# A mixture of experts that gathers its rows by tile of slots instead of scattering them into slots

## The chip, the cores and the metric

One program on one core of a Trainium2 chip. The metric is the device time of one execution in microseconds (us). The engines are TensorE (PE, whose weight loads have a row of their own, PEld), VectorE (DVE), ScalarE (ACT), GpSimd (POOL) and SyncE (SP, which here only issues DMAs).

## What is computed

A decoder of twelve sublayers over 8 sequences of 256 tokens with 256 features (2048 tokens in all). The change concerns the third sublayer, a mixture of 8 experts of which each token uses two. Cut to what matters:

```
S, C, K, E = 2048, 640, 2, 8                 # tokens, slots of an expert, choices, experts
probs = softmax(xf @ Wg)                     # 2048 x 8
top_vals, top_idx = top_k(probs, K)
onehot = one_hot(top_idx.T.reshape(-1), E)   # first choices of all tokens, then second choices
loc = place of each (token, choice) in its expert: cumsum(onehot) - 1
keep = loc < C
gates = top_vals * keep;  gates /= max(gates.sum(-1), 1e-9)
buf[e, loc] = xf[token]                      # 8 experts x 640 slots x 256
hid = buf @ W_in;  a, g = split(hid);  hid = gelu(a) * g
out_e = hid @ W_out
y[token] = sum over its two choices of gates * out_e[e, loc]
```

The sublayer is followed by a residual sum and a normalisation of each token's row.

## The kernel before

The sublayers run one after another, each in a block of its own (`turn`); x stays in SBUF twice, `x_tok` (a token in each partition, 16 tiles of 128 tokens) and `x_feat` (transposed). Within a block every engine has its own program in a fixed order, and semaphores connect them. `then(...)` makes VectorE wait for the end of the instruction it wraps before the next.

`mixture_top2` has three stretches. (1) Routing: TensorE makes the logits, VectorE the softmax, the two best experts, one-hot rows `hot` and, by two products with `ones16` and `before16` and a scan, the place of each of the 4096 (token, choice) pairs in its expert; at the end `slot` (128 partitions x 2 choices x 16 tiles of tokens) holds 640 * expert + place, or a number out of bounds where the expert is full (L1688, which raises `slot_done`). (2) The rows travel. ScalarE has copied x into `sheets`, two copies with rows of 258 words: 256 of x, the gate, and the pair's number. GpSimd issues 32 indirect DMAs (L1506), one for each choice and tile of tokens, that scatter 128 rows each into `rows_in` in HBM; SyncE waits until all 32 have landed (L1465) and loads the slots, one expert of five tiles a DMA (L1473), three experts ahead, into `xt`. (3) Experts: the 40 tiles of 128 slots go in 16 parts (`PARTS`, 3 and 2 tiles of an expert in turn). `turn_row` transposes a tile (L1528), ScalarE stores it in `xT` (L1605); `hidden` multiplies by `w_in` (L381 is the line of the helper `mm`), ScalarE makes gelu (L1613), VectorE the product with the gate half (L1695); `outer` multiplies by `w_out`, VectorE scales by the row's gate (L1703) and raises `out_stored`, and GpSimd scatters the 128 rows to `rows_back`, a row for each (token, choice) pair (L1513). In a part TensorE does `hidden` of part q, `outer` of part q-1 and `turn_row` of part q+1, so that a tile is transposed about five tiles before its own `outer`. A ring of `RING` = 4 buffers `y` holds results until their scatter has landed. When all 40 have, SyncE reads `rows_back` by token, two rows each, and the residual follows.

`rows_in` has to hold something in slots that no pair takes: the first sublayer's SyncE program writes 40 tiles of `ident` and of `blank` (whose last word is a pair number out of bounds) into it (L916, L918), then zeros into `rows_back` (L921), then issues the loads of the masks (L1284). `rows_in` is filled again in the fourth sublayer for the second mixture (`mixture_top3`), which is not changed but for the count that it waits for.

An fp32 matmul of the program is two matmul instructions in the trace, with a weight load each; a transpose is one.

## Time and profile before

| | us |
|---|---|
| median of 3 runs | 2690.61 (2690.55 to 2693.39) |
| the profiled execution | 2685.21 |
| its span, from first to last instruction | 2683.4 |
| TensorE busy | 2294.8 (86%) |
| VectorE busy | 1425.6 (53%) |
| ScalarE busy | 1041.7 (39%) |
| GpSimd busy | 700.3 (26%) |
| mean granted TensorE clock | 0.921 |
| the mixture's block | 235.1 to 561.1 |

What lies around the span is 1.8 us. The span is a sequence of blocks, so a microsecond taken from the path within one block moves all that follows.
### The profile page before, as it was taken

To read this page: it belongs to the slowest core of one execution; us is meant where nothing else is said; L and a number is where in the kernel's file an instruction comes from. 1 tells how busy PE (TensorE), PEld (TensorE's weight loads), DVE (VectorE), ACT (ScalarE), POOL (GpSimd) and SP (SyncE) were. 2 spreads that over 40 slices of the span, in tenths; PEclk is the share of its full clock that TensorE was granted. 3 is DMA by queue.
4 is the path that set the end of the run, shared out by engine and by line. 5 is a ranking of instruction groups with operands and counts; after the bars stand their busy time and mean duration, and the time that the engine had idled before them with its cause. 6 is when DMAs were issued, how large, how long until landed. Compare 5 with 4: busy or idle time off the path is not lost. (4 is left out here: it accounts for less than half of the span.)

```text
span 2683.4 us, 38848 instructions
## 1 busy us (share of the span) xinstructions
PE 2294.8 (86%) x12968; PEld 1648.2 (61%) x12968; DVE 1425.6 (53%) x4229; ACT 1041.7 (39%) x2653; POOL 700.3 (26%) x670
## 2 busy tenths in 40 slices
PE   7994499888869829995699799698999898999898
PEld 5773377665547518883388566464566676466676
DVE  3565022266758764556133667454776443777454
ACT  3442111145526510045044266343666432666432
POOL 1013311110024342311644100563433101433111
PEclk9996799989969959997899899799999999999899
DMA  9123211184000010030254311400000000000000
GB/s 235 33 94 139 78 51 43 39 155 23 1 6 1 1 49 11 1 131 6 95 153 120 116 25 25 159 1 32 1 1 1 1 1 1 1 1 1 20 24 20
DMA packets 112242, 127.38 MB, mean 47 GB/s; under 512 B 46515, under 2 KB 100021, under 8 KB 110256
## 3 DMA queue, kind: packets, MB, share of 16 engines
q1 hardware_dynamic: 103312, 103.91, 14.5%
q0 software_dynamic: 8736, 20.99, 2.1%
q8 instruction: 109, 1.79, 0.3%
q14 instruction: 85, 0.70, 0.1%
HBM read 79.93 MB, written 47.90 MB: 48 GB/s over the span
## 5 line engine op out<-in xcount | busy, mean ns | idle before, releaser
L381 PE MATMUL bank<-weights,work 128*128 128x256 f32 (+5 forms) x1768 | 467.3, 399 | 52.0 <-POOL work L2489 35.0
L381 PE MATMUL bank<-work,weights 128*128 128x256 f32 (+3 forms) x1680 | 407.5, 403 | 20.0 <-DVE work L4710 12.6
L381 PEld LDWEIGHTS bank<-weights,work 128*128 128x128 f32 (+2 forms) x1768 | 315.8, 192 | 151.5 <-issue 66.3
L381 PEld LDWEIGHTS bank<-work,weights 128*128 128x128 f32 (+1 forms) x1680 | 299.5, 189 | 101.2 <-DVE work L4710 16.1
L765 POOL TENSOR_TENSOR work<-work,minus_half 128x2 f32<-128x2 f32 x96 | 69.7, 726 | 837.0 <-DVE work L758 837.0
L381 PE MATMUL bank<-weights,x_feat 128*128 128x512 f32 (+2 forms) x576 | 213.0, 503 | 16.0 <-ACT weights L4286 10.0
L790 ACT COPY x_feat<-bank 128x512 f32<-128x512 f32 x80 | 46.5, 584 | 324.1 <-PE bank L782 323.7
L381 PEld LDWEIGHTS bank<-weights,x_feat 128*128 128x128 f32 x576 | 106.8, 198 | 74.8 <-issue 50.4
L4310 ACT ACTIVATE work<-work 128x128 f32<-128x128 f32 (+1 forms) x256 | 137.0, 543 | 1.7 <-DVE work L4397 1.7
L381 PE MATMUL bank<-x_feat,weights 128*128 128x256 f32 (+3 forms) x400 | 117.5, 471 | 19.9 <-PEq L232 15.2
L1695 DVE TENSOR_TENSOR work<-bank,work 128x384 f32<-128x384 f32 (+1 forms) x64 | 31.4, 491 | 189.5 <-ACT work L1613 189.5
L381 PE MATMUL bank<-weights 128*128 128x256 f32 (+1 forms) x560 | 125.9, 380 | 1.5 <-DVE weights L4427 0.9
L381 PEld LDWEIGHTS bank<-weights 128*128 128x128 f32 x560 | 105.0, 192 | 16.7 <-ACT weights L4334 1.3
L381 PEld LDWEIGHTS bank<-x_feat,weights 128*128 128x128 f32 (+1 forms) x400 | 78.1, 213 | 48.1 <-issue 22.8
L381 PE MATMUL bank<-work 128*128 128x256 f32 (+3 forms) x326 | 73.3, 362 | 29.5 <-ACT work L2875 7.8
L782 PE MATMUL bank<-ident,x_tok 128*128 128x128 f32 x320 | 61.4, 327 | 38.1 <-DVE x_tok L773 36.1
L4720 DVE SCALAR_TENSOR_TENSOR work<-bank,weights,work 128x256 f32<-128x256 f32 x96 | 45.6, 482 | 85.1 <-ACT work L4658 84.0
L4122 POOL TENSOR_TENSOR work<-work,minus_half 128x8 f32<-128x8 f32 x32 | 52.4, 1636 | 145.2 <-DVE work L4441 145.2
L1513 POOL DMA_INDIRECT rows_back<-work x40 | 38.9, 971 | 195.2 <-DVE work L1703 191.5
L4658 ACT ACTIVATE work<-bank,weights 128x256 f32<-128x256 f32 x80 | 37.9, 474 | 126.5 <-PE bank L381 126.3
L4389 DVE CUSTOM_DVE_ANT_0 work<-bank,work 128x128 f32<-128x128 f32 (+1 forms) x256 | 75.9, 352 | 16.9 <-PE bank L4173 16.9
L1613 ACT ACTIVATE work<-bank 128x384 f32<-128x384 f32 (+1 forms) x64 | 28.0, 437 | 146.3 <-PE bank L381 146.3
(465 smaller groups left out, 4688.8 us busy)
## 6 DMA issues: line engine op xcount, KB each, us to landing
weights<-in_weights SPq DMA_DIRECT2D x1, 12296.0 KB
weights<-in_weights SPq DMA_DIRECT2D x1, 9360.0 KB
weights<-in_weights SPq DMA_DIRECT2D x1, 8488.0 KB
work<-rows_in SPq DMA_DIRECT2D x62, 129.0 KB
rows_in<-ident SPq DMA_DIRECT2D x2, 3968.0 KB, 43.7
weights<-rows_back SPq DMA_DIRECT2D x8, 768.0 KB, 5.1
work<-rows_in SPq DMA_DIRECT2D x8, 645.0 KB, 4.2
rows_in<-ident SPq DMA_DIRECT2D x2, 2560.0 KB, 34.4
```

The source lines that it names most:

```text
L381: ins = nc.tensor.matmul(out, lhsT, rhs, start=(i == 0), stop=(i == len(pairs) - 1))
L765: nc.gpsimd.tensor_tensor(t.rstd[:, n, :], t.rstd[:, n, :], K.minus_half[:, 0:2], ALU.pow).then_inc(K.S.rstd_done, 1)
L782: ins = nc.tensor.transpose(K.bank[bank][:, (2 * k + i) * P:(2 * k + i + 1) * P], K.x_tok[:, 2 * b + i, k * P:(k + 1) * P], K.ident[:])
L790: copy(K.x_feat[:, :, b * L:(b + 1) * L], K.bank[bank][:, :].rearrange("p (k t) -> p k t", k=KT)).then_inc(K.S.xT_stored, 1)
L1513: nc.gpsimd.indirect_dma_start(K.rows_back, bass.IndirectOffsetOnAxis(ap=to, axis=0), y[:, r, :], None, bounds_check=TOP * T - 1, oob_is_e ...
L1613: nc.scalar.activation(gelu[:, at % 2, 0:n], K.bank[2 * (at % 2)][:, 0:n], ACT.Gelu).then_inc(S.gelu_done, 1)
L1695: nc.vector.tensor_tensor(hT[:, q % 2, m, 0:n], K.bank[2 * (at % 2) + 1][:, 0:n], gelu[:, at % 2, 0:n], ALU.mult).then_inc(S.inner_stored, 1)
L4122: nc.gpsimd.tensor_tensor(rk, norm[:, 1, :], K.minus_half[:, 0:H], ALU.pow).then_inc(S.rk_done, 1)
L4310: ins = nc.scalar.activation(probs[:, u % 3, s, at:at + width], probs[:, u % 3, s, at:at + width], ACT.Exp, bias=bias[:, u % 2, i, s:s + 1 ...
L4389: ins = nc.vector.tensor_tensor_reduce(probs[:, u % 3, s, at:at + width], K.bank[SM[s]][:, at:at + width], seen[:, at:at + width], 1.0, -3 ...
L4658: nc.scalar.activation(gelu[:, n % 2, :], K.bank[n % RING][:, L:2 * L], ACT.Gelu, bias=W["b1"][:, layer, HT + f:HT + f + 1]).then_inc(S.ge ...
L4720: nc.vector.scalar_tensor_tensor(out=hid[rows, b % 2, f, :], in0=K.bank[n % RING][rows, 0:L], scalar=W["b1"][rows, layer, f:f + 1], in1=ge ...
```

## The change

Rows are no longer scattered into slots. At the start of the block SyncE writes x twice into `slots_in` in HBM, a row for each (token, choice) pair (2 DMAs of 2048 KB, semaphore `x_doubled`). VectorE goes on from `slot`: it splits the number into the tile of slots (0 to 39) and the place in the tile (0 to 127), and makes one-hot rows of both, `in_tile` (128 x 32 x 40) and `in_slot` (128 x 32 x 128), and `value`, which is `in_tile` times the pair's number plus one (`ids`) and times its gate (`share`). TensorE adds up 32 products of `in_slot` (as weights) and `value` (80 columns) in one bank: the result says for each place and tile which pair sits there and with what gate. Six small VectorE operations turn it into `weight`, `source` (row to read, 0 where the slot is empty) and `target` (row to write, out of bounds where empty), and raise `slot_done`. GpSimd then gathers: one indirect DMA for each tile of slots from `slots_in` into one of `AHEAD` = 8 buffers `xt`; eight at once, and from then on gather j+8 behind scatter j. SyncE loads no slots, ScalarE makes no copies of x, and the fill of `rows_in` in the first sublayer is gone. Semaphores that even blocks share are assigned anew. The gate comes from `weight`.

```
     def sync(sp):
         follow_weights(sp, K, 0)
-        fill = K.rows_in[0:40 * P, :].rearrange("(n p) c -> p n c", p=P)
-        for k in range(KT):
-            sp.dma_start(fill[:, :, k * P:(k + 1) * P], K.ident[:].unsqueeze(1).broadcast_to([P, 40, P])
-                         ).then_inc(K.rows_cleared, 16)
-        sp.dma_start(fill[:, :, D:D + 2], K.blank[:].unsqueeze(1).broadcast_to([P, 40, 2])
-                     ).then_inc(K.rows_cleared, 16)
         sp.wait_ge(S.zeros_done, 1)
         sp.dma_start(K.rows_back[0:2 * T, :].rearrange("(n p) d -> p n d", p=P),
                      zeros.unsqueeze(1).broadcast_to([P, 2 * TILES, D])).then_inc(K.back_cleared, 16)
...
-    place, none, share, slot = A(TOP, TILES), A(TOP, TILES), A(TOP, TILES), A(TOP, TILES, dt=U32)
+    place, none, share = A(TOP, TILES), A(TOP, TILES), A(TOP, TILES)
+    slot, low, ids = A(TOP, TILES, dt=I32), A(TOP, TILES), A(TOP, TILES)
+    columns, tiles_of, found = A(P), A(E * EACH), A(2, E * EACH)
+    source, target, weight = A(E * EACH, dt=U32), A(E * EACH, dt=U32), A(E * EACH)
     tail = tail_buffers2(A)
     at = A.at
-    sheets = A(TOP, TILES, ROW)
+    in_tile, in_slot, value = A(TOP * TILES, E * EACH), A(TOP * TILES, P), A(TOP * TILES, 2, E * EACH)
     A.at = at
-    xt, xT, hT = A(SETS, EACH, ROW), A(2, KT, WIDE), A(2, HT, WIDE)
...
+    doubled = K.slots_in[0:TOP * T, :].rearrange("(i p c) d -> c p i d", p=P, c=TOP)
         def _(sp):
+            for c in range(TOP):
+                sp.dma_start(doubled[c], K.x_tok[:]).then_inc(K.x_doubled, 16)
             follow_weights(sp, K, 2)
-            sp.wait_ge(K.scattered_top2, 16 * TOP * TILES)
-            sp.wait_ge(S.x_copied, TOP)
-            slots = K.rows_in[0:E * CAPACITY, :].rearrange("(e i p) c -> e p i c", e=E, p=P)
-            for e in range(E):
-                if e >= SETS:
-                    for r in range(RING):
-                        done = len(range(r, EACH * (e - SETS + 1), RING))
-                        sp.wait_ge(K.sent_top2[r], 16 * done)
-                sp.dma_start(xt[:, e % SETS, :, :], slots[e]).then_inc(slots_loaded[e % SETS], 16)
...
-                ins = nc.gpsimd.iota(sheets[:, c, :, D + 1:D + 2].rearrange("p i a -> p (i a)").bitcast(U32),
-                                     pattern=[[TOP * P, TILES]], base=c, channel_multiplier=TOP)
-            ins.then_inc(S.pool_step, 1)
+                nc.gpsimd.iota(ids[:, c, :], pattern=[[TOP * P, TILES]], base=c + 1, channel_multiplier=TOP,
+                               allow_small_or_imprecise_dtypes=True)
+            nc.gpsimd.iota(tiles_of, pattern=[[1, E * EACH]], base=0, channel_multiplier=0,
+                           allow_small_or_imprecise_dtypes=True)
+            nc.gpsimd.iota(columns, pattern=[[1, P]], base=0, channel_multiplier=0,
+                           allow_small_or_imprecise_dtypes=True).then_inc(S.pool_step, 1)
+            def gather(j):
+                if j >= AHEAD:
+                    p.wait_ge(S.row_turned, j - AHEAD + 1)
+                nc.gpsimd.indirect_dma_start(xt[:, j % AHEAD, :], None, K.slots_in,
+                                             bass.IndirectOffsetOnAxis(ap=source[:, j:j + 1], axis=0),
+                                             bounds_check=TOP * T - 1, oob_is_err=False).then_inc(K.gathered[j % AHEAD], 16)
+
+            def scatter(j):
+                p.wait_ge(S.out_stored, j + 1)
+                nc.gpsimd.indirect_dma_start(K.rows_back, bass.IndirectOffsetOnAxis(ap=target[:, j:j + 1], axis=0),
+                                             y[:, j % RING, :], None, bounds_check=TOP * T - 1, oob_is_err=False
+                                             ).then_inc(K.sent_top2[j % RING], 16)
+
+            p.wait_ge(S.pool_step, 4)
+            p.wait_ge(K.back_cleared, 16)
+            p.wait_ge(K.x_doubled, 16 * TOP)
             p.wait_ge(S.slot_done, 1)
-            p.wait_ge(S.x_copied, TOP)
-            p.wait_ge(S.pool_step, 4)
-            p.wait_ge(K.rows_cleared, 48)
-            p.wait_ge(K.back_cleared, 16)
-            for c in range(TOP):
-                for i in range(TILES):
-                    nc.gpsimd.indirect_dma_start(K.rows_in, bass.IndirectOffsetOnAxis(ap=slot[:, c, i:i + 1], axis=0),
-                                                 sheets[:, c, i, :], None, bounds_check=E * CAPACITY - 1,
-                                                 oob_is_err=False).then_inc(K.scattered_top2, 16)
-            for j, (q, i) in enumerate(tiles):
-                r = j % RING
-                p.wait_ge(S.out_stored, j + 1)
-                to = row_of(q, i)[:, D + 1:D + 2].bitcast(U32)
-                nc.gpsimd.indirect_dma_start(K.rows_back, bass.IndirectOffsetOnAxis(ap=to, axis=0), y[:, r, :], None,
-                                             bounds_check=TOP * T - 1, oob_is_err=False).then_inc(K.sent_top2[r], 16)
+            for j in range(AHEAD):
+                gather(j)
+            for j in range(len(tiles)):
+                scatter(j)
+                if j + AHEAD < len(tiles):
+                    gather(j + AHEAD)
...
+                pe.wait_ge(K.gathered[j % AHEAD], 16 * (j // AHEAD + 1))
                 if j >= 2:
                     pe.wait_ge(S.row_stored, j - 1)
                 for k in range(KT):
-                    ins = nc.tensor.transpose(K.bank[6 + j % 2][:, k * P:(k + 1) * P], row_of(q, i)[:, k * P:(k + 1) * P],
+                    ins = nc.tensor.transpose(K.bank[6 + j % 2][:, k * P:(k + 1) * P], xt[:, j % AHEAD, k * P:(k + 1) * P],
                                               K.ident[:])
...
+            for n in range(TOP * TILES):
+                if n % TILES == 0:
+                    pe.wait_ge(S.row_found, n // TILES + 1)
+                ins = nc.tensor.matmul(K.bank[5][:, 0:2 * E * EACH], in_slot[:, n, :],
+                                       value[:, n, :, :].rearrange("p a j -> p (a j)"), start=n == 0,
+                                       stop=n == TOP * TILES - 1)
+            ins.then_inc(S.aux_done, 1)
             pe.wait_ge(S.slot_done, 1)
...
-            nc.scalar.copy(sheets[:, 0, :, 0:D], K.x_tok[:]).then_inc(S.x_copied, 1)
             a.wait_ge(S.max_done, 1)
             nc.scalar.activation(prob, prob, ACT.Exp).then_inc(S.probs_done, 1)
-            nc.scalar.copy(sheets[:, 1, :, 0:D], K.x_tok[:]).then_inc(S.x_copied, 1)
             for j in range(PARTS[0][2]):
...
-            for c in range(TOP):
-                ins = nc.vector.tensor_tensor(sheets[:, c, :, D:D + 1], share[:, c, :].unsqueeze(2), total.unsqueeze(2),
-                                              ALU.mult)
-            then(ins)
+            then(nc.vector.tensor_tensor(share, share, total.unsqueeze(1).broadcast_to([P, TOP, TILES]), ALU.mult))
             far = float(2 * E * CAPACITY)
             then(nc.vector.tensor_scalar(none, none, -far, far, ALU.mult, ALU.add))
             then(nc.vector.tensor_tensor(place, place, none, ALU.add))
             then(nc.vector.scalar_tensor_tensor(out=place, in0=by_rank(wheref), scalar=float(CAPACITY), in1=place,
                                                 op0=ALU.mult, op1=ALU.add))
-            nc.vector.tensor_copy(slot, place).then_inc(S.slot_done, 1)
+            then(nc.vector.tensor_copy(slot, place))
+            then(nc.vector.tensor_scalar(slot, slot, P - 1, None, ALU.bitwise_and))
+            then(nc.vector.tensor_copy(low, slot))
+            then(nc.vector.tensor_tensor(place, place, low, ALU.subtract))
+            then(nc.vector.tensor_scalar(place, place, 1.0 / P, None, ALU.mult))
+            both, ranks = [P, TOP * TILES, E * EACH], "p c i -> p (c i)"
+            then(nc.vector.tensor_tensor(in_tile, tiles_of.unsqueeze(1).broadcast_to(both),
+                                         place.rearrange(ranks).unsqueeze(2).broadcast_to(both), ALU.is_equal))
+            for n, x in enumerate((ids, share)):
+                nc.vector.tensor_tensor(value[:, :, n, :], in_tile, x.rearrange(ranks).unsqueeze(2).broadcast_to(both),
+                                        ALU.mult)
+            for c in range(TOP):
+                nc.vector.tensor_tensor(in_slot[:, c * TILES:(c + 1) * TILES, :],
+                                        columns.unsqueeze(1).broadcast_to([P, TILES, P]),
+                                        low[:, c, :].unsqueeze(2).broadcast_to([P, TILES, P]), ALU.is_equal
+                                        ).then_inc(S.row_found, 1)
+            v.wait_ge(S.aux_done, 4)
+            inverse = K.bank[5][:, 0:2 * E * EACH].rearrange("p (a j) -> p a j", a=2)
+            nc.vector.tensor_copy(weight, inverse[:, 1, :])
+            then(nc.vector.tensor_scalar(found[:, 0, :], inverse[:, 0, :], -0.75, 0.25, ALU.add, ALU.max))
+            then(nc.vector.tensor_copy(source, found[:, 0, :]))
+            then(nc.vector.tensor_scalar(found[:, 1, :], inverse[:, 0, :], 0.5, float(4 * T), ALU.is_lt, ALU.mult))
+            then(nc.vector.tensor_tensor(found[:, 1, :], found[:, 1, :], found[:, 0, :], ALU.add))
+            nc.vector.tensor_copy(target, found[:, 1, :]).then_inc(S.slot_done, 1)
...
-                nc.vector.tensor_scalar(y[:, j % RING, :], K.bank[4 + j % 2][:, 0:D], row_of(q, i)[:, D:D + 1], None,
+                nc.vector.tensor_scalar(y[:, j % RING, :], K.bank[4 + j % 2][:, 0:D], weight[:, j:j + 1], None,
...
-        K.slots_in = nc.dram_tensor("slots_in", (6400, D), F32, kind="Internal").ap()
+        K.slots_in = nc.dram_tensor("slots_in", (2 * T, D), F32, kind="Internal").ap()
```

How the instructions stand. VectorE, where the routing ends and the experts begin, before:

```order
L1680 TENSOR_TENSOR work<-work 128x16 x2
L1684 TENSOR_SCALAR work<-work 128x32
L1685 TENSOR_TENSOR work<-work 128x32
L1686 SCALAR_TENSOR_TENSOR work<-work 128x32
L1688 CAST work<-work 128x32
L1695 TENSOR_TENSOR work<-bank1,work 128x384
```

VectorE, from the same place on, of the changed kernel (bank 5 is where the 32 products are added up):

```order
L1682 CAST work<-work 128x32
L1683 TENSOR_SCALAR work<-work 128x32
L1684 CAST work<-work 128x32
L1685 TENSOR_TENSOR work<-work 128x32
L1686 TENSOR_SCALAR work<-work 128x32
L1688 TENSOR_TENSOR work<-work 128x1280
L1691 TENSOR_TENSOR work<-work 128x32x40 x2
L1694 TENSOR_TENSOR work<-work 128x2048 x2
L1700 COPY work<-bank5 128x40
L1701 TENSOR_SCALAR work<-bank5 128x40
L1702 CAST work<-work 128x40
L1703 TENSOR_SCALAR work<-bank5 128x40
```

Behind these stand two more of 128x40 and then the first product of the experts: 15 instructions more between the CAST of `slot` and the experts than before.

TensorE at the same place, before:

```order
L1571 MATMUL bank1<-ident,work 128x128 x4
L381 MATMUL bank3<-work 128x256
L381 MATMUL bank2<-work 128x256
L1528 MATMUL bank6<-ident,work 128x128 x2
L1528 MATMUL bank7<-ident,work 128x128 x2
```

and of the changed kernel:

```order
L1563 MATMUL bank1<-ident,work 128x128 x4
L381 MATMUL bank3<-work 128x256
L381 MATMUL bank2<-work 128x256
L1573 MATMUL bank5<-work 128x80 x32
L1520 MATMUL bank6<-ident,work 128x128 x2
L1520 MATMUL bank7<-ident,work 128x128 x2
```

The 32 products stand in a row between the routing's last products and the first transposes; from there on the two orders are the same.

GpSimd's whole list of row transfers before:

```order
L1506 DMA rows_in<-work 7936x258 x32
L1513 DMA rows_back<-work 6144x256 x40
L765 TENSOR_TENSOR work<-work,minus_half 128x2 x8
```

and its beginning in the changed kernel:

```order
L1485 IOTA work 128x128
L1490 DMA work<-slots_in,work 128x256 x8
L1496 DMA rows_back<-work 6144x256
L1490 DMA work<-slots_in,work 128x256
L1496 DMA rows_back<-work 6144x256
```

Eight gathers in place of 32 scatters stand ahead of the experts, and 32 more alternate with the first 32 of the 40 scatters of results.

## Rows read from the trace of the kernel before

**Rows 1.** The page's part 1: busy us (share of the span) xinstructions

```profile
PE 2294.8 (86%) x12968; PEld 1648.2 (61%) x12968; DVE 1425.6 (53%) x4229; ACT 1041.7 (39%) x2653; POOL 700.3 (26%) x670
```

**Rows 2.** Windows: engines' busy us, granted clock, DMA share, GB/s, by stretch

```profile
core 0: us, PE busy (x) PEld busy (x) DVE busy (x) ACT busy (x) POOL busy (x), PEclk, DMA share, GB/s
...
253.50:296.60 43.10, 0.00 (x0) 0.00 (x0) 0.00 (x0) 0.00 (x0) 31.36 (x32) 0.50 0.27 97
296.60:303.20 6.60, 1.81 (x7) 1.04 (x7) 0.00 (x0) 1.19 (x4) 0.00 (x0) 0.50 0.86 267
303.20:530.40 227.20, 219.19 (x906) 165.37 (x906) 50.80 (x104) 41.21 (x102) 38.86 (x40) 0.99 0.10 34
```

**Rows 3.** Timeline from `slot` to the experts: start us, us, engine, line, operation

```profile
253.26 0.18 DVE L1688 CAST work<-work 128x32 uint32<-128x32 f32 x1
254.35 1.22 POOL L1506 DMA_INDIRECT rows_in<-work  x1 [17.78 <-DVE work L1688]
255.88 0.98 POOL L1506 DMA_INDIRECT rows_in<-work  x1 [0.30 <-issue]
...
294.20 0.97 POOL L1506 DMA_INDIRECT rows_in<-work  x1 [0.30 <-issue]
296.63 1.50 SPq L1473 DMA_DIRECT2D work<-rows_in  x3
...
300.89 1.81 PE L1528 MATMUL bank<-ident,work 128*128 128x128 f32 x6 [53.09 <-DMA work<-rows_in]
...
303.16 7.21 PE L381 MATMUL bank<-work,weights 128*128 128x384 f32 x16 [0.46 <-ACT work L1605]
```

**Rows 4.** VectorE by width: timeline; last row busy us, mean ns

```profile
249.03 0.42 DVE L1666 TENSOR_TENSOR work<-work 128x256 f32<-128x256 f32 x1
...
253.01 0.21 DVE L1686 SCALAR_TENSOR_TENSOR work<-work 128x32 f32<-128x32 f32 x1
...
308.35 0.56 DVE L1695 TENSOR_TENSOR work<-bank,work 128x384 f32<-128x384 f32 x1 [54.92 <-ACT work L1613]
...
L3698 DVE TENSOR_REDUCE work<-weights 128x512 f32<-128x4096 f32 x1 | 4.4, 4416 | 0.0
```

**Rows 5.** Timeline of short TensorE pairs, at the lower and the upper clock

```profile
229.02 1.06 PE L782 MATMUL bank<-ident,x_tok 128*128 128x128 f32 x4
...
198.59 1.05 PE L381 MATMUL bank<-work 128*128 128x120 f32 x8
...
543.52 0.60 PE L782 MATMUL bank<-ident,x_tok 128*128 128x128 f32 x4
```

**Rows 6.** Windows where the granted clock (behind POOL) changes

```profile
304.00:306.00 2.00, 2.00 (x5) 1.09 (x4) 0.00 (x0) 0.41 (x1) 0.00 (x0) 0.50 0.00 0
306.00:307.00 1.00, 1.00 (x4) 0.56 (x3) 0.00 (x0) 0.00 (x0) 0.00 (x0) 0.60 0.00 0
...
532.00:533.00 1.00, 0.00 (x0) 0.00 (x0) 0.00 (x0) 0.00 (x0) 0.00 (x0) 0.54 0.90 315
```

**Rows 7.** The line of the scatters of results (L1513)

```profile
L1513 POOL DMA_INDIRECT rows_back<-work x40: 971/971/973, 320.7 to 528.2; - x40
...
DMA to landing us min/median/max: 2.0/2.4/4.1
```

**Rows 8.** Timeline: first result scaled; transposes of tile 8

```profile
319.47 0.48 DVE L1703 TENSOR_SCALAR work<-bank,work 128x256 f32<-128x256 f32 x1 [0.89 <-PE bank L381]
...
337.96 0.38 PE L1528 MATMUL bank<-ident,work 128*128 128x128 f32 x2
```

**Rows 9.** The DMAs' issues: count, KB each, us to landing

```profile
rows_back<-work SPq DMA_DIRECT2D x1, 4096.0 KB, 25.7
...
x_saved<-x_tok SPq DMA_DIRECT2D x1, 2048.0 KB, 9.1
```

**Rows 10.** Waits in 0 to 120 us: us in total, times, longest

```profile
PEld bank L381 <- DMA weights<-in_weights: 12.2, 1, 12.2
...
POOL x_tok L941 <- DMA ctx_feat<-in_ctx_feat: 5.2, 1, 5.2
```

40 lines of the change are left out of this document (17 added, 23 removed).

## The prediction

> **What bounds the kernel now.** TensorE is busy for 86% of the span [rows 1], so first I looked for places where it is not. The table of windows over this block shows one: from 253.5 to 296.6 us no TensorE, VectorE or ScalarE instruction runs, only GpSimd with its 32 scatters, and in the next 6.6 us TensorE is busy for 1.8 [rows 2]. From 303.2 on the experts keep TensorE at 219 of 227 us. So within this block two things set the time: the experts' products, which the change leaves as they are, and the way from the finished slot numbers to the first product of an expert. The timeline lays that way out [rows 3]: `slot` is ready at 253.26 + 0.18 = 253.44; the first scatter starts 0.91 later, the second 1.53 after it, the rest 1.28 apart (38.32 us over 30); the last starts at 294.20; SyncE issues the load of the slots 2.43 later; transposes begin at 300.89 and the first expert's product at 303.16. That is 49.7 us from `slot`, all of it on the path, for TensorE's transposes wait for nothing else (53.1 us, the one wait on a DMA). The question is what the new way from 253.44 costs.
>
> **Step 1, VectorE makes one-hot rows.** The nearest rows for small operations are those of 32 columns: 0.18 us and 0.04 to the next, so 0.22 [rows 4]. Four of them: 0.9. The gate's two operations become one, worth under 0.1, left out. The wide ones go by their length: 256 columns take 0.42, 384 take 0.56, and the one long row, 4096 columns, 4.42 [rows 4]. Between them the slope is 1.04 to 1.09 ns for a column, with 0.15 us on top. One of 1280 columns is 1.5 us and there are three (`in_tile`, two `value`): 4.5; one half of `in_slot`, 2048 columns, is 2.3. TensorE may begin when the first half stands: 253.44 + 0.9 + 4.5 + 2.3 + 0.1 of gaps = 261.2. The second half ends at 263.5, under TensorE's first. Bounds: the long row is a reduction and not two operands that are spread out, but 4.42 / 4096 leaves little room below; above, I allow 2 us.
>
> **Step 2, TensorE adds up 32 products.** That is 64 weight loads of 128 columns and 64 matmuls of 80. No row has this shape. The nearest have 128 and 120 columns behind loads of 128: four take 0.60 us at the upper clock, eight take 1.05, so one more costs 0.11; four take 1.06 at the lower clock, so about 0.21 [rows 5]. With 128 columns loaded and 128 streamed in 0.107, load and stream run beside each other; with 80 streamed the load of 128 should set the pace, still 0.107. The clock: TensorE has then been idle for some 13 us and starts at the lower level. In the trace it began at 300.89 and was at 1.2 GHz until within 306 to 307 (mean 0.60 there) [rows 3, 6], 5.5 us. The same again gives 25 pairs at 0.21 (5.3 us), then 39 at 0.107 (4.2), and 0.2 until the last is out: 9.7, ending at 270.9. Ends: 7 us if the 80 streamed columns set the pace (0.067, by the 0.107 for 128), 13.7 + 0.2 if the clock stays low.
>
> **Step 3, six small VectorE operations** of 40 columns, in a chain: 6 x 0.22 = 1.3, so `slot_done` at 272.2.
>
> **Step 4, the gathers.** The trace has no gather; the nearest row is the scatter of as many rows. From VectorE's end to the first indirect DMA 0.91 us, to the third another 1.53 + 1.28 [rows 3]: it starts at 275.9. A scatter lands 2.0 to 4.1 us after its issue, 2.4 in the median [rows 7]: 278.3. Then two transposes, a copy by ScalarE and the product; before, three tiles took 303.16 - 300.89 = 2.3 for that, and now two of them are done while the third travels. I take 1.2 (between 0.8 and 2.3). First product at 279.5 instead of 303.2.
>
> **The gain is 23.7 us.** What else moves:
> - The two copies of x to HBM. They are issued at the block's start, 235.1. Copies of 2048 KB have landed after 9.1 us, one of 4096 KB after 25.7 [rows 9]; 235.1 + 18.2 = 253 or 235.1 + 25.7 = 261 stands against a need at 272.2. Cost nothing; covered by the routing and steps 1 to 3, with 11 us to spare, and from then on one for one. Behind them on SyncE's queue stands the load of the fourth sublayer's weights, needed at 561.
> - ScalarE's two copies of x (3.6 us each) lay beside the routing: nothing. Three more iotas on GpSimd lie there too.
> - The fill of `rows_in` in the first sublayer, 5 MB, goes. Nothing there waits for a DMA after 12.2 us but GpSimd's first bias addition, 5.2 us, for an input that was issued ahead of the fill [rows 10]; TensorE and VectorE wait for no transfer. It gains nothing, and zeros and masks land earlier than they are needed.
> - In the experts GpSimd issues 72 indirect DMAs instead of 40. Results are scaled from 319.47 on [rows 8], one in 5.3 us on average (to 527.0, 39 steps), and two issues take 2 x 1.28 = 2.6. A gather stands behind the scatter of eight tiles earlier: that of tile 8 may be issued at about 319.95 + 1.3 + 1.3 in old times, lands by 327 even at 4.1, and its transposes stand at 337.96 [rows 8]: 11 us to spare. The ring of four results can take a scatter that lands 1.3 us later. SyncE's loads of slots are off no one's path. Nothing.
> - The clock at the first expert. Before, TensorE ran 3.2 us of the product at the lower clock (303.16 to 306.4). Now it rests for about 5 us after step 2, and 5 us of rest took it down elsewhere (TensorE's last product of the experts ends at 527, mean 0.54 in 532 to 533 [rows 6]), so it begins low again, for 1.5 to 5.4 us: between 0.8 better and 1.1 worse, taken as nothing.
>
> So the profiled execution's 2685.2 would become 2661.5; it lies 5.4 below the median of the unprofiled runs, against which I forecast: 2690.6 - 23.7 = 2666.9, a gain of 0.9%.
>
> **A rule of the Trainium skill, and the first rival.** The profile's own rows are those above: eight load and stream pairs in 1.05 us, where loads and streams one after another would need 8 x (0.107 + 0.100) = 1.66 [rows 5]. The Trainium skill, page TensorE: Matmul & The Clock Gate, section Part 3: Packing small matmuls, states that weight loads overlap running matmuls only when they address other row groups. All 64 here use the whole array. By that rule the pairs would not overlap; the trace disagrees, for its pairs use the whole array too. As a rival nonetheless: if in this sum the pairs run one after another, each costs 0.107 + 0.067 = 0.174 at the upper and 0.35 at the lower clock: 5.3 us for 15, then 49 x 0.174 = 8.5, so 14.0 instead of 9.7, and the time is 2671.2. I give it 0.12, since here both operands were just written and no row shows 80 columns.
>
> **The other rivals.**
> - Gathers are dearer than scatters, for the issue or for landing. If each of the first three costs 1.5 us more on GpSimd and the last lands after 4.1, this adds 3 x 1.5 + 1.7 = 6.2: 2673.1. The trace speaks neither for nor against; 0.08.
> - The copies of x come late, as two of 25.7 us one behind the other: 235.1 + 51.4 = 286.5 instead of 272.2, so 2681.2, still faster. The 9.1 us row speaks against it; 0.04.
> - Slower than before: GpSimd cannot keep up. Its list is strict, and each tile wants a scatter and a gather within 5.3 us. Scatters take 0.97 with no spread (971 to 973 ns over 40, beside VectorE at work [rows 7]). The point from which it decides is a gather of 5.3 - 1.3 = 4.0 us; at 5.5 us the 32 gathers in the experts would hold them back by 32 x 1.5 = 48, and the first three by 13: 2690.6 - 23.7 + 61 = 2728. The Trainium skill, page SBUF — State Buffer, section SBUF: two separate sides, names a mechanism: VectorE copies from SBUF to SBUF in fp32 keep GpSimd from writing descriptors of its DMAs; in the experts VectorE reads PSUM in each operation, so that rule would not bite. 0.04.
> - The gain is given back, within 0.2% of before: the experts' stretch, now at a mean granted clock of 0.99 behind one at 0.50 [rows 2], would have to slow by a tenth once TensorE no longer rests 53 us ahead of them. Nothing in the trace hints at it; 0.03.
> - Better than the forecast's own range: the clock stays high through the wait for the gathers, the 80 columns set the pace, and the first sublayer gains from free DMA engines, together more than 6 us: below 2661. 0.03.
>
> **How the numbers follow.** Forecast 2666.9, with a range of its own of 2661 to 2671 (step 2 from -2.7 to +4.2, landing -0.4 to +1.7, clock -0.8 to +1.1, VectorE up to +2, of which hardly all fall on one side): 0.66. With the first two rivals 0.86; the range for them is 2661 to 2676. A measurement of this kernel tells about 0.2% (5.4 us) from no change. Faster by over that, below 2685.2: 0.66 + 0.12 + 0.08 + 0.04 + 0.03 = 0.93. Same: 0.03. Slower: 0.04.
>
> **What would show each step.** In the profile of the changed kernel: VectorE's row of 1280 columns at 1.5 us and of 2048 at 2.3; TensorE's 64 matmuls of 80 columns from about 261 to 271, with the pace going from 0.21 to 0.11 where the clock rises; first gather near 273; GpSimd's gathers at 0.97 us; TensorE's wait on a DMA falling from 53.1 us to some 5; first expert's product near 279.5, and from there to the block's end the same 258 us as before. Wrong if transposes in the experts wait for gathers, if scaled results wait for scatters, if the first gather waits for `x_doubled`, or if the first sublayer's length changes by more than 1 us.

## The result, and the profile after

| | before | changed |
|---|---|---|
| median (range) | 2690.58 us (2686.32 to 2693.39) | 2667.28 us (2664.14 to 2675.13) |
| ratio, 95% interval | | 0.9919 (0.9893 to 0.9945) |
| the profiled execution | 2685.21 | 2675.13 |
| its mixture block, mark to mark | 325.9 | 308.3 |
| all its other blocks together | 2351.6 | 2359.0 |

The change is faster by 0.8%, 23.3 us between the medians; 23.7 were forecast. The profiled executions are only 10.1 apart, and that of the changed kernel is the slowest of its four. A block's length is read between two marks on GpSimd (L238, an instruction at each block's start; 232.19 and 558.09 before, 233.07 and 541.40 now). The gain lies in the mixture's block, 17.6 us, and part of it is missing again elsewhere in this execution. The page's part 1, of the changed kernel, answers to [rows 1]:

```profile
PE 2323.4 (87%) x13032; PEld 1669.3 (62%) x13032; DVE 1434.8 (54%) x4243; ACT 1036.5 (39%) x2651; POOL 712.3 (27%) x680
```

The timeline of the changed kernel from `slot` to the experts answers to [rows 3] (start us, us, engine, line, operation, in brackets the idle time before it and who ended it):

```profile
254.05 0.18 DVE L1682 CAST work<-work 128x32 int32<-128x32 f32 x1
...
255.14 1.49 DVE L1688 TENSOR_TENSOR work<-work 128x1280 f32<-128x1280 f32 x1
256.67 2.89 DVE L1691 TENSOR_TENSOR work<-work 128x1280 f32<-128x1280 f32 x2
259.48 4.48 DVE L1694 TENSOR_TENSOR work<-work 128x2048 f32<-128x2048 f32 x2
...
261.82 13.94 PE L1573 MATMUL bank<-work 128*128 128x80 f32 x64 [13.15 <-DVE work L1694]
275.79 0.20 DVE L1700 COPY work<-bank 128x40 f32<-128x40 f32 x1 [11.83 <-PE bank L1573]
...
276.82 0.18 DVE L1705 CAST work<-work 128x40 uint32<-128x40 f32 x1
278.01 1.30 POOL L1490 DMA_INDIRECT work<-slots_in,work  x1 [40.30 <-DVE work L1705]
279.62 1.00 POOL L1490 DMA_INDIRECT work<-slots_in,work  x1 [0.30 <-issue]
280.93 1.00 POOL L1490 DMA_INDIRECT work<-slots_in,work  x1 [0.31 <-issue]
...
283.78 0.69 PE L1520 MATMUL bank<-ident,work 128*128 128x128 f32 x2 [0.59 <-DMA work<-slots_in,work]
...
284.93 8.22 PE L381 MATMUL bank<-work,weights 128*128 128x384 f32 x16 [0.46 <-ACT work L1604]
```

`slot` stands at 254.05 + 0.18 = 254.23, the first product of an expert at 284.93: 30.7 us, where it was 49.7. In order: VectorE's one-hot rows until TensorE may start, 7.6; the products, 13.94; VectorE's six small operations, 1.2; 1.0 to the first gather; 2.9 to the third; 2.85 until it has landed and its transposes begin; 1.15 until the product. The products are the long piece. The window over them (engines' busy us, then the granted clock, DMA share and GB/s), changed kernel:

```profile
261.80:278.00 16.20, 13.94 (x64) 13.73 (x64) 3.24 (x7) 0.00 (x0) 0.00 (x0) 0.50 0.00 0
```

64 load and stream pairs in 13.94 us are 0.218 each, and the granted clock is 0.50 (1.2 GHz) all the way, although TensorE is busy without a gap. The gathers and the scatters of results, by line (duration ns min/median/max, first and last start; last row from issue to landing of the gathers), and what TensorE waits for in the block:

```profile
L1490 POOL DMA_INDIRECT work<-slots_in,work x40: 997/1025/1299, 278.0 to 474.8; - x40
...
DMA to landing us min/median/max: 2.7/2.9/3.6
```

```profile
L1496 POOL DMA_INDIRECT rows_back<-work x40: 980/1021/1024, 303.5 to 511.0; - x40
```

```profile
PE bank L1573 <- DVE work L1694: 13.1, 1, 13.1
...
PE bank L1520 <- DMA work<-slots_in,work: 6.7, 3, 5.5
```

A gather takes 1.0 us of GpSimd as a scatter did [rows 7], the first one 1.30. TensorE waits three times for gathers, and these are the first three tiles; the 53.1 us of [rows 3] are gone, and in the experts no transpose waits for one.

### The profile page after: what moved, and what is told of

Same layout as the page of the kernel before. It is cut to its first block and busy times, and to the rows that moved or that the text cites. A ratio compares the mean times of both kernels' runs of the same rounds, so it can differ in the third digit from the quotient of the medians.

```text
span 2673.3 us, 39009 instructions
## 1 busy us (share of the span) xinstructions
PE 2323.4 (87%) x13032; PEld 1669.3 (62%) x13032; DVE 1434.8 (54%) x4243; ACT 1036.5 (39%) x2651; POOL 712.3 (27%) x680
## 5 line engine op out<-in xcount | busy, mean ns | idle before, releaser
L381 PE MATMUL bank<-weights,work 128*128 128x256 f32 (+5 forms) x1768 | 468.6, 400 | 53.1 <-POOL work L2506 35.0
L381 PE MATMUL bank<-weights,x_feat 128*128 128x512 f32 (+2 forms) x576 | 215.1, 508 | 16.3 <-ACT weights L4303 10.1
L773 DVE TENSOR_SCALAR x_tok<-x_tok,work 128x256 f32<-128x256 f32 x192 | 77.6, 447 | 11.6 <-POOL work L765 11.5
L3110 POOL DMA_INDIRECT rows_back<-work x62 | 60.3, 973 | 86.7 <-DVE work L3371 83.1
```

Of the source, the lines that this page charges most:

```text
L381: ins = nc.tensor.matmul(out, lhsT, rhs, start=(i == 0), stop=(i == len(pairs) - 1))
L773: ins = nc.vector.tensor_scalar(x, x, t.mv[:, b % 2, i, 0:1], t.rstd[:, b % 2, i:i + 1], ALU.subtract, ALU.mult)
L3110: nc.gpsimd.indirect_dma_start(K.rows_back, bass.IndirectOffsetOnAxis(ap=to, axis=0), y[:, r, :], None, bounds_check=TOP * T - 1, oob_is_e ...
```

## Experiments

All run against the kernel before on the same chip, its executions spread among theirs: `again`, `fill_back`, `chunks` and `warm` together on one chip, `again_2`, `before_again`, `fill_back_2` and `chunks_warm` on a second, `warm_short` and `ahead6` on a third, without the changed kernel beside them. Block lengths are from mark to mark of the profiled execution, and the other blocks are those between its first and its last mark; "products" are the 64 pairs of L1573.

| kernel | median us (range), executions | ratio (95%) | profiled | products begin, last | mixture block | other blocks |
|---|---|---|---|---|---|---|
| changed | 2667.28 (2664.14–2675.13), 4 | 0.9919 (0.9893–0.9945) | 2675.13 | 261.82, 13.94 | 308.3 | 2359.0 |
| again | 2669.65 (2658.10–2674.92), 6 | 0.9924 (0.9905–0.9942) | 2665.86 | 259.41, 13.95 | 306.1 | 2352.0 |
| again_2 | 2666.53 (2663.13–2670.63), 5 | 0.9914 (0.9899–0.9929) | 2667.20 | 259.46, 13.94 | 306.2 | 2353.3 |
| fill_back | 2660.39 (2660.15–2663.73), 4 | 0.9894 (0.9880–0.9908) | 2660.57 | 259.50, 13.94 | 306.1 | 2346.7 |
| fill_back_2 | 2663.60 (2659.73–2669.17), 5 | 0.9908 (0.9891–0.9925) | 2663.10 | 262.05, 13.94 | 306.2 | 2349.1 |
| warm | 2670.05 (2665.17–2676.58), 6 | 0.9927 (0.9914–0.9939) | 2670.36 | 267.36, 7.27 | 309.0 | 2353.6 |
| warm_short | 2663.35 (2653.83–2664.46), 4 | 0.9905 (0.9888–0.9922) | 2653.83 | 260.17, 7.37 | 300.1 | 2345.9 |
| chunks | 2662.84 (2655.99–2664.22), 4 | 0.9892 (0.9877–0.9906) | 2663.88 | 255.67, 13.94 | 303.3 | 2352.8 |
| chunks_warm | 2658.89 (2656.81–2660.00), 4 | 0.9883 (0.9868–0.9899) | 2660.00 | 258.04, 9.41 | 296.2 | 2356.0 |
| ahead6 | 2671.55 (2668.56–2673.14), 4 | 0.9930 (0.9914–0.9947) | 2673.14 | 259.68, 13.94 | 309.1 | 2356.3 |
| before_again | 2687.40 (2683.93–2692.49), 10 | 1.0000 (0.9989–1.0011) | 2685.08 | | 326.2 | 2350.6 |

The last column is the noise of this kernel: the same instructions outside the block (but for the fill) take 2346 to 2359 us. So what an edit does within the block is read from the block; the medians carry the rest. The block has a noise of its own: five traces of code that is the same within it gave 306.1 to 306.2 four times and 308.3 once.

### again, again_2, before_again: the same kernels once more

The changed kernel and the kernel before, unchanged.

> The changed kernel once more, nothing edited, for a second trace and a narrower interval. Both theories: VectorE's row of 1280 columns 1.5 us, gathers 1.0 us each, from the end of the cast of `slot` to the first expert's product 26 to 31 us (49.7 in the kernel before). Theory A (the path is the sum of its steps, and the 32 products run at 0.218 us a pair because the granted clock stayed at 0.50): if the clock stays low again, 64 pairs take 13.9 us; if it rises within, less, down to 9.7. Theory B (the executions differ in other blocks): the blocks around differ by up to 5 us from the first trace with the same instructions. Time 2664 to 2672.

> The changed kernel a third time, beside fill_back_2, since the changed kernel came out at 2669.7 us in the median and the one with the fill put back at 2660.4, against both theories. Theory A (the two differ only by which executions had the clock low in other blocks): both medians within 3 us of each other this time, 2660 to 2670, mixture's block 306 to 309 us in both. Rival (the fill's absence costs something): the changed kernel 5 us or more above fill_back_2 again.

> The kernel before, nothing edited, for a second trace of it. Theory A (blocks with the same instructions differ by the granted clock from execution to execution): the mixture's block takes 325 to 327 us again, within 1.5 us, and others differ from the first trace by up to 5 us; the second mixture's block (274.2 us in the first trace, 275.3 to 279.2 in five traces of changed kernels) falls anywhere in 274 to 279. Rival (the change made the second mixture's block 4 us slower): 274 to 275 again.

Measured: blocks of 306.1, 306.2 and 326.2 us, so 19.7 to 20.1 between the kernels where the first pair of traces gave 17.6. The difference between the two readings is the first expert's 16 matmuls. TensorE's timeline there, of `again` (compare 8.22 above, and 7.21 in [rows 3]):

```profile
259.41 13.95 PE L1573 MATMUL bank<-work 128*128 128x80 f32 x64 [13.13 <-DVE work L1694]
...
282.49 6.61 PE L381 MATMUL bank<-work,weights 128*128 128x384 f32 x16 [0.46 <-ACT work L1604]
```

From `slot` to this product `again` has 251.83 to 282.49 = 30.66, the same as the 30.70 above. What differs most is when the granted clock rises (1.6 us of the 2.2 between the two blocks). Over its 15 executions in the three jobs the changed kernel spreads from 2658.1 to 2675.1, median 2666.5.

### fill_back, fill_back_2: the fill of the first sublayer

```diff
     def sync(sp):
         follow_weights(sp, K, 0)
+        fill = K.rows_in[0:40 * P, :].rearrange("(n p) c -> p n c", p=P)
+        for k in range(KT):
+            sp.dma_start(fill[:, :, k * P:(k + 1) * P], K.ident[:].unsqueeze(1).broadcast_to([P, 40, P])
+                         ).then_inc(K.rows_cleared, 16)
+        sp.dma_start(fill[:, :, D:D + 2], K.blank[:].unsqueeze(1).broadcast_to([P, 40, 2])
+                     ).then_inc(K.rows_cleared, 16)
...
-            sp.wait_ge(K.rows_cleared, 48)
+            sp.wait_ge(K.rows_cleared, 96)
```

> The fill of 40 tiles of `rows_in` put back into the first sublayer, all else as changed. Theory A (the whole gain is in the mixture's block): no difference to the changed kernel beyond 1 us in the first block (232 to 233.5 us) and a time within 3 us of it. Rival B (a part of the gain came from taking 5 MB of writes away): the first block 2 us or more longer and the time 2 to 6 us above the changed kernel.

> The fill of the first sublayer put back, a second time. Theory A: within 3 us of again_2. Rival (leaving the fill away costs time, by some change of the clock or of where blocks begin): 5 us or more below it, 2658 to 2662.

SyncE's timeline in the first sublayer, `fill_back`:

```profile
13.00 17.63 SPq L916 DMA_DIRECT2D rows_in<-ident  x1
30.66 15.19 SPq L918 DMA_DIRECT2D rows_in<-blank  x1
```

Its queue is held for 32.8 us by the fill, and nobody else waits longer. The first block is 228.2 us with it (230.6 in the second run), 228.1, 228.1 and 230.6 without; the mixture's block is 306.1 and 306.2 either way. The medians, 2660.4 and 2663.6 with the fill against 2669.7 and 2666.5 without, lean the other way, and the first pair, 9.3 apart, fits neither theory. Pooled they are 2663.1 (9 executions) and 2666.5 (15), and the intervals of the ratio overlap in both comparisons. One block sets the traces apart, the one behind the second mixture: 183.6 to 184.0 us in all four traces with the fill (the two of the kernel before among them), 184.7 to 187.5 in the eight without. They differ there in the granted clock (in its second 10 us 0.92 to 0.94 with the fill, 0.61 to 0.97 without), and nothing in the traces ties that to the fill. So: removing the fill shows no gain, as forecast; whether it costs some 3 us is open.

### warm: extra products ahead of the 32, to raise the clock

```diff
+            for _ in range(22):
+                mm(nc, K.bank[4][:, :], [(K.ident[:], K.x_feat[:, 0, 0:512])])
             for n in range(TOP * TILES):
                 if n % TILES == 0:
                     pe.wait_ge(S.row_found, n // TILES + 1)
```

> 22 extra fp32 products of the identity with 512 columns of x, into a bank that is free, ahead of the 32 products, so that TensorE is not idle while VectorE makes the one-hot rows. Their results are not used. Theory A (the 14 us of the 32 products are the low clock, with load and stream of a pair beside each other): the granted clock is 1.00 when they start, a pair takes 0.107 us, 64 take 6.9, and the first expert's product comes 7 us earlier; time 5 to 8 us below the changed kernel. Rival (weight load and stream of a pair one after another, 0.174 us at the upper clock): 64 take 11.1 us and the gain is 2.8 us. Rival (the pace is set by something that no clock changes): 13.9 us as before, no gain.

TensorE's timeline of `warm`, and windows across it (the clock is the number behind POOL's):

```profile
246.12 21.40 PE L381 MATMUL bank<-x_feat,ident 128*128 128x512 f32 x44
267.36 7.27 PE L1575 MATMUL bank<-work 128*128 128x80 f32 x64
280.11 0.66 PE L1520 MATMUL bank<-ident,work 128*128 128x128 f32 x2 [5.48 <-DMA work<-slots_in,work]
...
283.72 7.73 PE L381 MATMUL bank<-work,weights 128*128 128x384 f32 x16 [0.46 <-ACT work L1606]
```

```profile
248.00:250.00 2.00, 2.00 (x4) 0.84 (x3) 1.85 (x6) 0.00 (x0) 0.00 (x0) 0.50 1.02 431
250.00:251.00 1.00, 1.00 (x2) 0.34 (x1) 0.86 (x5) 0.00 (x0) 0.00 (x0) 0.57 0.95 406
251.00:252.00 1.00, 1.00 (x4) 0.47 (x3) 0.83 (x5) 0.00 (x0) 0.00 (x0) 1.00 0.09 33
...
278.00:280.00 2.00, 0.00 (x0) 0.00 (x0) 0.00 (x0) 0.00 (x0) 1.39 (x3) 0.54 0.22 66
```

The extra products are 44 pairs, the clock was at 2.4 GHz from 251 on, and then the 64 pairs of the change took 7.27 us, 0.114 each, and 13.95 at 1.2 GHz. That settles what the pair costs: load and stream overlap at either clock. One behind the other they would need 0.174 each, 11.1 us (the first rival's price). The Trainium skill, page TensorE: Matmul & The Clock Gate, section Part 3: Packing small matmuls, states in its list of what overlaps that a weight load overlaps running matmuls only where row groups differ. These 64 all use the whole array, the trace has 0.114 a pair, and so it disagrees with that rule as the list puts it; a sentence ahead of the list allows a load into a background weight buffer too, and with that one the trace is in accord.

The run as a whole gained nothing (its block is 309.0, 2.9 longer than that of `again`, where a time 5 to 8 us lower was expected), and this was my sizing: a pair of 512 columns costs 0.43 at the upper clock, so 22 products last too long. They end at 267.4, where the operands of the change had been ready since 259.4 or so, and the shorter products end at 274.6, after the 273.4 of `again`. Then, in the wait for the gathers, the clock went down again (0.54 in 278 to 280).

### warm_short: 12 extra products instead of 22

The same edit with `range(12)`.

> As `warm`, with 12 extra products instead of 22, which at the 0.854 us (upper clock) to 1.7 us (lower) of one end at about 259.4, when the first half of the one-hot rows is ready, instead of at 267.4. Results not used. Theory A (low clock, pairs overlap): the 32 products take 7.1 us (0.111 a pair) and end near 266.6 instead of 273.4; the first expert's product comes 6.5 to 7 us before that of the changed kernel, its own clock low at first; the mixture's block 299 to 300.5 us against 306.1; time 4 to 8 us below the changed kernel. Rival (the extra products cost as much as they give, or the clock drops between them): block over 303 us.

Timeline of `warm_short`, TensorE's work and VectorE's cast of `slot`, and the window over the 64 pairs:

```profile
246.81 13.23 PE L381 MATMUL bank<-x_feat,ident 128*128 128x512 f32 x24
...
252.40 0.18 DVE L1684 CAST work<-work 128x32 int32<-128x32 f32 x1
...
260.17 7.37 PE L1575 MATMUL bank<-work 128*128 128x80 f32 x64
273.06 0.66 PE L1520 MATMUL bank<-ident,work 128*128 128x128 f32 x2 [5.52 <-DMA work<-slots_in,work]
...
276.65 6.91 PE L381 MATMUL bank<-work,weights 128*128 128x384 f32 x16 [0.46 <-ACT work L1606]
```

```profile
260.10:267.60 7.50, 7.37 (x64) 7.22 (x64) 2.24 (x3) 0.00 (x0) 0.00 (x0) 1.00 0.01 2
```

The extras end as the operands become ready. The 64 pairs take 7.37 us at a granted clock of 1.00 and end at 267.5 instead of 273.4. From `slot` (252.58) to the first expert's product it is 24.1 us instead of 30.7, 6.6 less, and the block is 300.1 instead of 306.1 to 306.2; the rest is `slot`, 0.2 later in the block, and the first 16 matmuls, 0.3 longer than in `again`. So the low clock under the 32 products costs 6 us of the block. The forecast had counted 2.6 of them, with 25 pairs at the low clock; that it was all 64 is what term 2 lacked. The medians don't show the gain by themselves: 0.9905 (0.9888 to 0.9922) overlaps the 0.9914 (0.9899 to 0.9929) of `again_2`.

### chunks: the one-hot rows in four pieces

```diff
-            then(nc.vector.tensor_tensor(in_tile, tiles_of.unsqueeze(1).broadcast_to(both),
-                                         place.rearrange(ranks).unsqueeze(2).broadcast_to(both), ALU.is_equal))
...
+            both = [P, FOUND, E * EACH]          # FOUND = 8
+            for h in range(TOP * TILES // FOUND):
+                part = slice(h * FOUND, (h + 1) * FOUND)
+                then(nc.vector.tensor_tensor(in_tile[:, part, :], tiles_of.unsqueeze(1).broadcast_to(both),
+                                             place.rearrange(ranks)[:, part].unsqueeze(2).broadcast_to(both), ALU.is_equal))
...
-                if n % TILES == 0:
-                    pe.wait_ge(S.row_found, n // TILES + 1)
+                if n % FOUND == 0:
+                    pe.wait_ge(S.row_found, n // FOUND + 1)
```

> The one-hot rows are made in four pieces of 8 (token tile, choice) pairs, each with its `in_tile`, `value` and `in_slot`, and TensorE starts behind the first piece. Same arithmetic, eight VectorE instructions more. Theory A: TensorE's products start 3.5 to 4 us earlier (piece: 0.5 + 2 x 0.5 + 1.2 = 2.7 us in place of 6.7 until the first half), take the same 13.9 us since VectorE's 2.7 us a piece stays under TensorE's 3.5, and the first expert's product comes 4 us earlier; time 4 us below the changed kernel. Rival (VectorE, not TensorE, sets the pace of this stretch): TensorE waits for VectorE at each piece and the gain is under 2 us.

Timeline of `chunks`, VectorE's cast of `slot` and TensorE's products:

```profile
251.97 0.18 DVE L1683 CAST work<-work 128x32 int32<-128x32 f32 x1
...
255.67 13.94 PE L1574 MATMUL bank<-work 128*128 128x80 f32 x64 [9.07 <-DVE work L1697]
...
278.80 7.27 PE L381 MATMUL bank<-work,weights 128*128 128x384 f32 x16 [0.46 <-ACT work L1605]
```

From the end of `slot` (252.15) to the products it is 3.5 us instead of 7.6, and TensorE never waits between the pieces: VectorE needs 2.46 for one, TensorE 3.5 at the low clock. The first expert's product starts 30.66 - (278.80 - 252.15) = 4.0 earlier after `slot` than in `again`. The block is shorter by 2.8 to 2.9: the first 16 matmuls took 7.27 here and 6.61 there, `slot` itself came 0.2 later in the block, and 0.3 lies behind the 16. The median, 2662.84, is 6.8 below that of `again` on the same chip, where 4 were expected; the intervals of the two ratios overlap by a hair (0.9906 and 0.9905).

### chunks_warm: both, and products in the wait for the gathers

`chunks`, with 8 extra products ahead of the 32 and 6 behind them:

```diff
             ins.then_inc(S.aux_done, 1)
+            for _ in range(6):
+                mm(nc, K.bank[4][:, :], [(K.ident[:], K.x_feat[:, 0, 0:512])])
             pe.wait_ge(S.slot_done, 1)
```

> The four pieces of `chunks`, 8 extra fp32 products of 512 columns ahead of the 32 products (sized by the 0.854 us that one took in `warm`, so that they end when the first piece is ready) and 6 more behind them, while the gathers travel; results not used. Theory A (the path is the sum of its steps, and the clock is what made the products 14 us): products at 0.11 us a pair and paced by VectorE's pieces of 2.5 us, from about 256 to 265 in the time of `chunks`, where they ended at 269.6; the clock is 1.00 at the first expert's product, which saves another 1.5 to 3; together 6 to 8 us below chunks and 10 to 12 below the changed kernel in the mixture's block (296 us). Rival (clock falls in the wait for the gathers all the same): 4 to 5 us below chunks.

TensorE's timeline of `chunks_warm`, and windows at the rise of the clock:

```profile
258.04 2.01 PE L1576 MATMUL bank<-work 128*128 128x80 f32 x16
260.51 2.01 PE L1576 MATMUL bank<-work 128*128 128x80 f32 x16 [0.46 <-DVE work L1701]
...
265.44 2.01 PE L1576 MATMUL bank<-work 128*128 128x80 f32 x16 [0.45 <-DVE work L1701]
267.29 5.36 PE L381 MATMUL bank<-x_feat,ident 128*128 128x512 f32 x12
...
276.38 5.43 PE L381 MATMUL bank<-work,weights 128*128 128x384 f32 x16 [0.46 <-ACT work L1609]
```

```profile
250.00:252.00 2.00, 2.00 (x3) 0.67 (x2) 1.86 (x6) 0.00 (x0) 0.00 (x0) 0.50 0.91 382
252.00:254.00 2.00, 2.00 (x4) 0.86 (x3) 1.73 (x9) 0.00 (x0) 0.00 (x0) 0.61 0.81 343
254.00:256.00 2.00, 2.00 (x6) 0.90 (x5) 1.72 (x9) 0.00 (x0) 0.00 (x0) 1.00 0.00 0
...
272.60:276.00 3.40, 1.33 (x7) 0.60 (x6) 0.00 (x0) 0.79 (x3) 2.77 (x3) 1.00 0.34 102
```

Each quarter of the products now takes 2.01 us and TensorE waits 0.46 for the next: with the clock up, VectorE sets the pace. With the 12 extra pairs behind, the clock stayed at 1.00 over the wait, and the first 16 matmuls of the experts took 5.43, against 6.61 to 8.28 in the traces without them. The block is 296.2, ten less than the changed kernel's and 7.1 less than that of `chunks`, as expected. The median, 2658.89, is below that of both kernels: on the same chip the changed kernel ran in 2666.53, and the two intervals of the ratio only touch, at 0.9899. The price is 14 products whose results nobody reads.

### ahead6: six gathers ahead instead of eight

```diff
-    E, TOP, HT, AHEAD = 8, 2, 4, 8
+    E, TOP, HT, AHEAD = 8, 2, 4, 6
```

> AHEAD = 6 instead of 8, so that gather j+6 stands behind scatter j. Theory A (gathers have some 11 us to spare at 8, two tiles are 10.6 of it): at 6 the gather of the third tile of a part is issued behind the scatter two steps ahead of its transposes and lands about when they are due, so TensorE waits 0 to 0.5 us seven times: the mixture's block 306 to 310 us, time 0 to 3 us above the changed kernel. Rival (GpSimd is already near its limit in the experts): waits of 2 us and more at most tiles, block over 315 us.

The transposes' line (idle before them in us, times, weight loads and matmuls together), first of `ahead6`, then of `again`; below it the waits of matmuls and of weight loads on gathers within the experts of `ahead6`, and the first product there:

```profile
  DMA work<-slots_in,work: 11.4, 13
```

```profile
  DMA work<-slots_in,work: 8.6, 5
```

```profile
PE bank L1520 <- DMA work<-slots_in,work: 0.2, 1, 0.2
```

```profile
PEld bank L1520 <- DMA work<-slots_in,work: 2.4, 7, 0.6
```

```profile
282.84 8.28 PE L381 MATMUL bank<-work,weights 128*128 128x384 f32 x16 [0.46 <-ACT work L1604]
```

With two tiles less of a lead, gathers come late within the experts. Seven weight loads wait for one, 2.4 us in all and 0.6 at most, as often as was expected; the matmuls wait once, 0.2 us. In `again`, with eight ahead, nothing in the experts waits for a gather, so the eight of the change have slack, and GpSimd keeps up. Most of the block of 309.1 does not come from this: of the 3.0 us to `again`, the first 16 matmuls took 1.7 (8.28, with the granted clock at 0.82 in 282 to 300 against 0.92), 0.1 lay ahead of them and 1.2 behind. Of the 1.2 the first trace of the changed kernel has 0.7 too, with its eight ahead, so the late gathers cost 1.2 us at most. The median of 2671.55 is 5.0 above that of the changed kernel's 15 executions, none of them taken beside it, where 0 to 3 were expected, and within their range (2658.1 to 2675.1); the medians decide nothing here.

## Why the prediction was right, and where it was not

- **What bounds the kernel now.** Right. The whole gain is in the stretch between `slot` and the first expert: 49.7 us became 30.7, 19.0 less, with the first 16 matmuls 1.0 longer in this trace (18.0 of the block's 17.6) and 0.6 shorter in `again` (19.6 of 19.7 to 20.1).
- **Step 1** (7.8 until TensorE may start): 7.6. 1280 columns took 1.49 and 2048 took 2.24, as their lengths said.
- **Step 2** (9.7): 13.94, the term that was mis-sized. The pair's two prices were right, 0.218 and 0.114 where 0.21 and 0.107 were forecast. Wrong was "The same again gives 25 pairs at 0.21": the granted clock was to rise after 5.5 us as it did behind the transposes [rows 6], and it stayed at 0.50 (1.2 GHz) for all 64, 13.94 us, in each of the seven traces without extra products. The range had this case as its end (13.7 + 0.2).
- **Step 3** (1.3): 1.2. **Step 4** (0.9, 2.8, 2.4, 1.2): 1.0, 2.9, 2.85, 1.15. Landing took 0.45 longer than the scatters' median.
- **The sum** for the stretch was 26.1 us and the trace has 30.7, so the forecast of the gain was 4.6 too high in the place where it was made. Yet the medians differ by 23.3, as forecast. That is luck in part. The same pair of kernels gave 19.9 us beside `again` and 22.3 beside `again_2`, and over all executions 22.7 (47 of the kernel before, median 2689.2; 15 of the changed one, 2666.5), while the blocks give 17.6 to 20.1. Two facts bear on it: both profiled executions of the kernel before (2685.21 and 2685.08) lie 2.3 to 5.4 us under its medians (2687.40 and 2690.58), so its other executions lose that somewhere, while those of the changed kernel (2675.13, 2665.86, 2667.20) lie on both sides of theirs. The forecast for the profiled execution was 2661.5, and all three are above it, by 4.4 to 13.6. The mean granted clock goes with the time from execution to execution (in `again` the changed kernel has 0.928 at 2658.10 us and 0.920 at 2672.95 and 2674.16), but in which block the unprofiled executions of the kernel before lose their 2 to 5 us, and whether the change takes that away, no trace shows. It stays open, and the closeness of the forecast to the median owes as much to it as to the steps.
- **Free things.** The two copies of x landed 7.8 and 14.1 us after their issue at 236.0 to 236.4, so by 250.5, long before the first gather; no wait names them. The fill and GpSimd's 72 issues cost and gave nothing that the traces show.
- **The clock at the first expert** was taken as nothing, between 0.8 better and 1.1 worse: 1.0 worse in the first trace, 0.6 better in the next two.
- **Rivals.** Load and stream one after another: refuted by `warm`, 7.27 us. It would have given nearly the time that was seen for the wrong reason: 14.0 us at a rising clock against 13.94 at a low one; only the granted clock of the stretch tells them apart. Dear gathers: 0.1 us more than the first scatter had for the first (1.30 and 1.22), 0.05 more for the others (medians 1.025 and 0.971). Late copies of x: no. GpSimd as the bound: no, a gather is 1.0 us, far from the 4.0 at which it would decide. Given back in the experts: not there, for from the 16 first matmuls to the end of the block it is 247.7 us before and 248.3, 247.6 and 247.6 in the three traces of the changed kernel.
- **Outside the block**, where the prediction expected nothing. In the second mixture's block, whose code is the same but for one count, the clock rises later than before. TensorE's timeline there, first before, then `again`; and what its transposes wait for, in the same order:

```profile
1276.87 8.01 PE L381 MATMUL bank<-weights,work 128*128 128x256 f32 x24
```

```profile
1250.38 12.52 PE L381 MATMUL bank<-weights,work 128*128 128x256 f32 x24
```

```profile
L3158 PE MATMUL bank<-ident,work 128*128 128x128 f32 x57 | 11.3, 285 | 22.4 <-DMA work<-rows_in 22.4
```

```profile
L3175 PE MATMUL bank<-ident,work 128*128 128x128 f32 x76 | 15.4, 288 | 16.5 <-DMA work<-rows_in 16.0 <-issue 0.4
```

  These 24 matmuls took 12.52 us in all three traces of the changed kernel, 8.01 before, and 8.01 again in `chunks`, whose code there is that of the changed kernel; so the code does not decide it. It costs little, for TensorE then waits for a DMA, and by 6 us less: the block is 274.2 and 277.2 before, 275.8 to 279.2 after. The 274.2 of the first trace did not come again in `before_again`, and over all other blocks the kernel before (2350.6 and 2351.6) lies within the 2345.9 to 2359.0 of the changed ones, so that the change loses time there is not shown.

## What to carry to other kernels

When work is moved onto an engine that has just rested, cost it at both clock levels and take the window's granted clock, not the busy share, as the witness: here TensorE was at 100% and at half speed. A wait of TensorE on something slow is also the place where its speed for the work behind is decided (the first 16 matmuls took 5.43 us behind a filled wait in `chunks_warm`, 6.91 behind an empty one in `warm_short`); work that nobody needs, ended just as the real operands arrive, gave 6 us of 306, and the same work sized too long gave nothing; each is one trace. Where single executions of one kernel spread by 17 us, measure an edit by the length of its block, and see whether the medians agree.

## What the runs showed of the hardware that I had not expected

- 64 pairs of a 128-column load and an 80-column stream cost 0.218 us each at a granted clock of 0.50 and 0.114 at 1.00. TensorE was busy for all of 13.9 us and the clock did not rise, in seven of seven traces without extra products. With pairs of 512 columns ahead it did rise while they ran (they began at 246.12 in `warm`, with 0.57 in 250 to 251, at 246.81 in `warm_short`, with 0.91 in 252 to 254, and at 248.74 in `chunks_warm`, with 0.61 in 252 to 254). Which difference between the two kinds of products decides this was not tried and is open.
- Rows gathered from HBM by an indirect DMA, 128 of 1 KB: 1.0 us on GpSimd, 0.3 to the next, landed 2.7 to 3.6 us after the issue (median 2.9), against 2.4 in the median for the scatters of 128 results of 1 KB in the kernel before.
- The same block of the same code differs by up to 5 us from one execution to the next with the moment at which the granted clock rises (the fourth block took 165.3 us in `again` and 170.1 in `again_2`; in its first 14 us the mean granted clock was 0.72 in the one and 0.50 in the other, in the next 14 us 1.00 and 0.81). That is more than the 2.8 us that `chunks` took off its block.
